# Moving the side work of four token tiles between ScalarE, VectorE and GpSimd in a two-layer kernel, and starting row scores two places sooner

## The reference, cut to what matters

```python
x = x + tanh(g_xattn[0]) * align(ctx_1024, layernorm(x))       # time warping against 1500 rows of a context
x = x + tanh(g_ffn[0])   * memory(layernorm(x), w_q, keys, w_down, w_up)
x = x + tanh(g_xattn[1]) * attention(layernorm(x), ctx_1024, ctx_1024, Wq, bq, Wk, bk, Wv, bv, Wo, bo)
x = x + tanh(g_ffn[1])   * experts(layernorm(x), W_router, b_router, W1, b1, W2, b2)

# memory: 8 heads, product keys (2 x 32), the best of 1024 experts each
h = einsum('bnd,bnhkd->bnhk', x, w_down[indices])
h = gelu(h, approximate=False) * relu(scores)
y = einsum('bnhk,bnhkd->bnd', h, w_up[indices])
# attention: 16 heads of 8, 56 queries against 1500 keys of the same batch
attn = softmax(einsum('bhqd,bhkd->bhqk', Q, K) / sqrt(8)); y = einsum('bhqk,bhkd->bhqd', attn, V) @ Wo + bo
```

## Time and profile before

| | us |
|---|---|
| median of three runs | 536.01 (534.08 to 536.66) |
| profiled execution | 540.89, of which the span from first to last instruction is 539.1 |
| PE busy | 435.2 (81%) |
| DVE busy | 366.1 (68%) |
| ACT busy | 281.9 (52%) |
| POOL busy | 86.0 (16%) |

### The profile page before, as it was taken

The page is one execution under the profiler, slowest core; times in us unless marked ns, Lnnn a source line. Parts: engine busy times, 40 slices in busy tenths (PEclk is TensorE's granted clock), DMA queues, the critical chain, the costliest instruction groups (busy, mean ns, idle before and its releaser), DMA issues.

```text
span 539.1 us, 10292 instructions
## 1 busy us (share of the span) xinstructions
PE 435.2 (81%) x4039; PEld 264.2 (49%) x4039; DVE 366.1 (68%) x1008; ACT 281.9 (52%) x491; POOL 86.0 (16%) x105
## 2 busy tenths in 40 slices
PE   3997888667888887257577568999989999989996
PEld 1343333335555574135445435666656566544443
DVE  7557999998666795868864757778869883371112
ACT  4365888755422591524245216466746567634443
POOL 2000000000000007777502602021010211100000
PEclk9999999998999999569797859799999999989999
DMA  8500565334522105486100780346273481000000
GB/s 287 213 2 0 154 195 163 118 101 122 170 68 64 52 3 117 113 203 150 34 1 1 162 183 2 72 103 149 53 146 85 90 283 34 2 0 0 1 0 18
DMA packets 28720, 50.07 MB, mean 93 GB/s; under 512 B 2464, under 2 KB 18400, under 8 KB 28672
## 3 DMA queue, kind: packets, MB, share of 16 engines
q1 hardware_dynamic: 26848, 45.74, 31.5%
q0 software_dynamic: 1536, 3.67, 2.7%
q10 hardware_dynamic: 288, 0.00, 0.0%
HBM read 39.96 MB, written 9.45 MB: 92 GB/s over the span
## 4 chain that ended last, share of the span: by engine, by line
PE 51%; DVE 30%; issue 6%; DMA 4%; POOL 4%; ACT 4%; SPq 1%; DVEq 0%; POOLq 0%
PE banks L1720 8%; PE banks L1696 8%; PE banks L1768 6%; PE banks L1832 5%; DVE arena L1320 5%; DVE work L1349 4%; PE banks L1846 4%; DVE mx L1103 3%; DVE arena L1373 2%; DMA arena<-key_parts 2%; PE banks L1408 2%; PE banks L1546 2%; PE banks L1662 2%; DVE work L1315 2%; PE banks L1412 2%
## 5 line engine op out<-in xcount | busy, mean ns | idle before, releaser
L1103 DVE TENSOR_REDUCE mx<-banks 112x1 f32<-112x500 f32 x168 | 107.9, 676 | 35.1 <-PE banks L1696 34.5
L851 ACT ACTIVATE arena<-banks 128x896 f32<-128x896 f32 x96 | 87.9, 916 | 69.1 <-PE banks L1768 68.0
L1696 PE MATMUL banks<-ctxT,arena 128*112 128x500 bf16 x144 | 56.4, 412 | 9.5 <-DVE mx L1103 6.6
L1720 PE MATMUL banks<-arena 128*32 128x112 f32 (+1 forms) x1536 | 60.6, 275 | 4.2 <-issue 3.3
L1430 PE MATMUL banks<-steps,one 128*128 128x500 f16 (+1 forms) x149 | 42.3, 357 | 11.1 <-DVE hcol L1049 10.5
L1720 PEld LDWEIGHTS banks<-arena 128*32 128x32 f32 (+1 forms) x1536 | 35.4, 112 | 25.6 <-issue 22.9
L1768 PEld LDWEIGHTS banks<-arena,ctxT 128*128 128x128 bf16 (+1 forms) x576 | 40.5, 110 | 12.0 <-issue 5.5
L1768 PE MATMUL banks<-arena,ctxT 128*128 128x112 bf16 (+1 forms) x576 | 44.6, 223 | 0.0
L1349 DVE SCALAR_TENSOR_TENSOR work<-twice,banks,arena 128x202 f32<-128x202 f32 x68 | 29.5, 434 | 18.8 <-PE banks L1546 18.8
L1320 DVE TENSOR_TENSOR_SCAN arena<-work,arena 128x100 f32<-128x100 f32 x70 | 29.8, 426 | 7.4 <-ACT work L663 5.0
L1469 PE MATMUL banks<-arena,minusb 128*128 128x375 bf16 x64 | 20.0, 331 | 17.8 <-ACT arena L672 15.0
(11 more groups left out here) (288 smaller groups left out, 760.5 us busy)
## 6 DMA issues: line engine op xcount, KB each, us to landing
ctxT<-key_parts SPq DMA_DIRECT2D x36, 375.0 KB, 6.3
key_parts<-arena SPq DMA_DIRECT2D x32, 281.2 KB, 2.8
ctxT<-in_ctx_T SPq DMA_DIRECT2D x12, 500.0 KB, 9.0
arena<-key_parts SPq DMA_DIRECT2D x12, 375.0 KB, 7.5
ctxT<-in_ctx_nat SPq DMA_DIRECT2D x5, 750.0 KB
arena<-in_ctx_nat SPq DMA_DIRECT2D x3, 750.0 KB
arena<-in_L_ffn_W SPq DMA_DIRECT2D x1, 2048.0 KB, 9.1
arena<-in_fold_w SPq DMA_DIRECT2D x1, 768.0 KB, 5.7
```

The source lines that it names most:

```text
L851: nc.scalar.activation(Pt[0:rows, g % 2, :].rearrange("p (a n) -> p a n", a=2), banks[0:rows, 2 + 2 * (g % 2):4 + 2 * (g % 2), 0:HQ // 2], ...
L1103: nc.vector.tensor_reduce(mx3[:, b % 2, u // NPIECE, u % NPIECE:u % NPIECE + 1], ps[k % 2][0:2 * NJ, 0:PIECE], AX_X, ALU.max).then_inc(s_m ...
L1696: nc.tensor.matmul(ps[k % ring][0:2 * NJ, 0:PIECE], QP[:, u // NPIECE, b, :], KP[b % 3][:, u // NPIECE, (u % NPIECE) * PIECE:(u % NPIECE + ...
L1720: last = nc.tensor.matmul(ps[6 + b % 2][q:q + 32, o:o + 2 * NJ], vals[0:rows, v0:v0 + 32], Pt[0:rows, g % 2, 2 * t * NJ:2 * (t + 1) * NJ], ...
```

## The change

- POOL clears `picks` where it filled the ones below key parts 0; ACT fills those ones instead of those below key parts 1, and lays `picks`, which DVE did. POOL fills the ones of key parts 1 later. Row scores no longer read the rows of ones (96 partitions instead of 128), so only the chunks wait for them.
- DVE lays the gates of tiles 0 and 1 in one operation each, where ACT did it in eight. The order on DVE becomes: tokens of tile 0, products of tile 1, query split of tile 0.
- Tiles 0 and 1 get their deviation from ACT's square root and DVE's reciprocal; ACT loads the tables of Sqrt and Gelu in turn for that. Tiles 2 and 3 get moments and a first guess on DVE, twelve Newton operations and the normalization on POOL.
- POOL splits the queries of tiles 1 to 3.
- Gelu of tiles 2 and 3 comes before the table of Exp, their memory output after chunk 2; the query rows of tile 1 come in chunks 5 to 8 of batch 0.
- `LEAD` is 6.

```diff
     MAXROW_AT = 10
-    LEAD = 4
+    LEAD = 6
     MAXROW = [NCH - 1] + (NB - 1) * [MAXROW_AT]
     DUE = [min(2 * g + 4, UNITS) if g < NCH else min(UNITS + 3 * (g - NCH + 1), 2 * (g + 1) + LEAD, (NB - 1) * UNITS)
            for g in range(NB * NCH)]
     assert all(DUE[b * NCH + MAXROW[b] - 1] >= (b + 1) * UNITS for b in range(NB - 1))
-    DOT_AT, GATE_AT, TOK_AT = (3, 6), 10, 18
-    NORM_AT, SPLIT_AT = (0, 2), 20
-    TURN_C, QUERY_C, LAY_C = 5, 7, 5
-    GELU_C, MEMORY_C = 4, 8
+    N_ROOT = 12
+    GATE_AT, TOK_AT, STAT_AT = 1, 10, 12
+    MEMORY_C, TURN_C, QUERY_C, LAY_C = 2, 5, 7, 5
...
-            nc.gpsimd.memset(ctxT[NPR:P, 0:KPW], 1.0 + 0x3F80 / 2.0 ** 23).then_inc(s_one[0], 1)
-            pool.wait_ge(s_one[0], 1)
+            nc.gpsimd.memset(picks, 0.0).then_inc(s_pz, 1)
+            pool.wait_ge(s_pz, 1)
...
+            def split_queries(i, t, nt):
+
+                q = Qm[:, 0:nt, :]
+                pool.wait_ge(s_qh, i + 1)
+                nc.gpsimd.tensor_tensor(q, q, QS[:, t:t + nt, 0, :], ALU.subtract).then_inc(s_rt, 1)
+                pool.wait_ge(s_rt, 1 if i == 1 else N_ROOT + 3)
+                nc.gpsimd.tensor_copy(QS[:, t:t + nt, 1, :], q).then_inc(s_rt, 1)
+                pool.wait_ge(s_rt, 2 if i == 1 else N_ROOT + 4)
+                nc.gpsimd.tensor_tensor(QS[:, t:t + nt, 2, :], q, QS[:, t:t + nt, 1, :], ALU.subtract).then_inc(s_qs, 1)
+
+            pool.wait_ge(s_gm, 2)
+            split_queries(1, 1, 1)
...
+            nc.gpsimd.memset(ctxT[NPR:P, KPW:2 * KPW], 1.0 + 0x3F80 / 2.0 ** 23).then_inc(s_one[1], 1)
+            pool.wait_ge(s_one[1], 1)
+            pool.wait_ge(s_vr, 3)
+            half, y, a = (ln[:, 2:4, i] for i in (8, 9, 10))
+            roots = 2
+
+            def root(ins):
+                nonlocal roots
+                roots += 1
+                ins.then_inc(s_rt, 1)
+                pool.wait_ge(s_rt, roots)
+
+            for _ in range(3):
+                root(nc.gpsimd.tensor_tensor(a, y, y, ALU.mult))
+                root(nc.gpsimd.tensor_tensor(a, a, half, ALU.mult))
+                root(nc.gpsimd.tensor_scalar(a, a, 1.5, None, ALU.subtract))
+                root(nc.gpsimd.tensor_tensor(y, y, a, ALU.mult))
+            for t in (2, 3):
+                if t == 3:
+                    pool.wait_ge(s_x2, 3)
+                nc.gpsimd.tensor_scalar(x_tok[:, t, :], x1_tok[:, t, :], ln[:, t, 6:7], ln[:, t, 9:10], ALU.subtract,
+                                        ALU.mult).then_inc(s_x2, 1)
+            pool.wait_ge(s_x2, 4)
...
+                if b == 1:
+                    split_queries(2, 2, 2)
+                    pool.wait_ge(s_qs, 3)
...
+            nc.scalar.activation(ctxT[NPR:P, 0:KPW], two1[NPR:P, 0:1].broadcast_to([P - NPR, KPW]), ACT.Copy
+                                 ).then_inc(s_one[0], 1)
+            act.wait_ge(s_pz, 1)
+            own = ident[:, :].rearrange("p (m r) -> p m r", r=G)
+            for c, (_, qx) in enumerate(PRODUCTS):
+                nc.scalar.activation(picks[:, :, qx, c::len(PRODUCTS)], own, ACT.Copy).then_inc(s_picks, 1)
...
+            gelu(0)
+            nc.scalar.activation(warm[:, 2:3], epsc[:, :], ACT.Sqrt)
+            token_deviation(0)
+            nc.scalar.activation(warm[:, 3:4], epsc[:, :], ACT.Gelu)
+            lay_tokens(0, 0, ps[7])
+            mask_queries(0, 0, ps[6])
+            gelu(1)
+            for p in range(NH // 4):
+                query_rows(0, p)
+            nc.scalar.activation(warm[:, 4:5], epsc[:, :], ACT.Sqrt)
+            token_deviation(1)
+            nc.scalar.activation(warm[:, 5:6], epsc[:, :], ACT.Gelu)
+            lay_tokens(1, 1, ps[7])
+            mask_queries(1, 1, ps[6])
...
-            nc.scalar.activation(warm[:, :], epsc[:, :], ACT.Exp)
             maxima_rows(0)
+            gelu(2)
+            gelu(3)
+            nc.scalar.activation(warm[:, 6:7], epsc[:, :], ACT.Exp)
...
-                    if b == 0 and c == GELU_C:
-                        gelu(2)
-                        gelu(3)
-                        nc.scalar.activation(warm[:, :], epsc[:, :], ACT.Exp)
...
-                    if b in (2, 3) and LAY_C <= c < LAY_C + NH // 4:
-                        query_rows(b, c - LAY_C)
+                    if b in (0, 2, 3) and LAY_C <= c < LAY_C + NH // 4:
+                        query_rows(b or 1, c - LAY_C)
...
+            def lay_gates(t):
+                ve.wait_ge(s_hs, t + 1)
+                nc.vector.tensor_tensor(
+                    diag[t], ident[0:TT, 0:TT].unsqueeze(1).broadcast_to([TT, NHK, TT]),
+                    hcol[:, t, :].unsqueeze(2).broadcast_to([TT, NHK, TT]), ALU.mult).then_inc(s_dg, 1)
+
+            def token_moments(t):
+                link(nc.vector.bn_stats(ln[:, t, 0:6], x1_tok[:, t, :]))
+                return nc.vector.bn_aggr(ln[:, t, 6:8], ln[:, t, 0:6])
...
+                ve.wait_ge(s_sr, t + 1)
+                link(nc.vector.reciprocal(ln[:, t, 9:10], ln[:, t, 8:9]))
+                nc.vector.tensor_scalar(x_tok[:, t, :], x1_tok[:, t, :], ln[:, t, 6:7], ln[:, t, 9:10], ALU.subtract,
+                                        ALU.mult).then_inc(s_x2, 1)
...
+            def guess_roots():
+
+                var, half, y = (ln[:, 2:4, i] for i in (7, 8, 9))
+                link(nc.vector.tensor_scalar(half, var, EPS, 0.5, ALU.add, ALU.mult))
+                nc.vector.tensor_scalar(y.bitcast(I32), half.bitcast(I32), -0.5, -554214945.0, ALU.mult, ALU.add
+                                        ).then_inc(s_vr, 1)
...
                 gates(0)
-                lay_picks()
+                lay_gates(0)
                 ve.wait_ge(s_x1c, 2)
                 add_memory(0)
+                token_moments(0).then_inc(s_vr, 1)
                 normalize_tokens(0)
-                split_queries(0, 0)
                 down(1)
+                split_queries()
+                gates(1)
+                ve.wait_ge(s_up, 1)
+                lay_gates(1)
...
                     reduce_pair(m)
-                    if m == 1:
-                        gates(1)
                     if m == 3:
                         add_memory(1)
+                        token_moments(1).then_inc(s_vr, 1)
+                    if m == 4:
                         normalize_tokens(1)
-                    if m == 5:
-                        split_queries(1, 1)
                 for step in range(7):
                     ve.wait_ge(s_dve, n)
                     split_maxima(0, step)
+                sum_dots(2)
+                sum_dots(3)
                 for k in range(UNITS, NB * UNITS):
                     b, u = k // UNITS, k % UNITS
-                    if b == 1 and u in DOT_AT:
-                        sum_dots(2 + DOT_AT.index(u))
                     if b == 1 and u == GATE_AT:
                         gates(2)
                         gates(3)
                     if b == 1 and u == TOK_AT:
                         add_memory(2)
                         add_memory(3)
-                    if b == 2 and u in NORM_AT:
-                        normalize_tokens(2 + NORM_AT.index(u))
-                    if b == 2 and u == SPLIT_AT:
-                        split_queries(2, 2)
+                    if b == 1 and u == STAT_AT:
+                        link(token_moments(2))
+                        link(token_moments(3))
+                        guess_roots()
                     reduce_scores(b, u)
...
                 if u == 0:
                     for half in range(2):
                         pe.wait_ge(s_kpl[b % 3][half], 16 * len(PRODUCTS) // 2 * (b // 3 + 1))
-                    if b < 3:
-                        pe.wait_ge(s_one[b], 1)
...
-            pe.wait_ge(s_qs, 2)
-            for p in range(NH // 4):
-                query_rows(1, p)
-            pe.wait_ge(s_qpa, NH // 2)
+            pe.wait_ge(s_qh, 2)
+            pe.wait_ge(s_xl, 2)
...
+                    if b == 0 and LAY_C <= c < LAY_C + NH // 4:
+                        pe.wait_ge(s_qs, 2)
+                        pe.wait_ge(s_vr, 3)
+                        query_rows(1, c - LAY_C)
```

110 lines of the change are left out of this document (42 added, 68 removed).

## The result

The changed kernel took 522.13 us in the median of four runs (518.82 to 522.59), the kernel before 536.34 on the same chip (534.08 to 539.32): ratio 0.973 [0.967, 0.979]. That is 14.2 us less; 23.7 were forecast. A second set of runs on another chip gave 522.48 beside 537.41, 14.9 less; its six runs spread from 513.53 to 526.51.

What follows compares the result with a forecast made beforehand. PE was taken as bound by waits for DVE's maxima, a table load and key parts, with half clock behind the gaps. Savings 6.2 + 5.2 + 5.0 + 5.6 + 1.7 = 23.7 us gave median 512.3, range 503 to 526.

Steps and rivals of the forecast that it cites:

- first rival: POOL's work holds up DVE at tile 1's norm, batch 0's split maxima and boundary casts: six us, 518; chance 0.15.
- half clock: PE stays at half clock through batch 1, 38.8 us instead of 25.8: 525; chance 0.12.
- A: From the gathers to batch 0's split maxima: earlier gathers and work taken off DVE save 6.2 us, between 1.5 and 7.5.
- B: Batch 0 and just ahead of it: waits, half clock and filling matmuls go, query rows of tile 1 enter; 5.2 us saved.
- C: Boundary from batch 0 to 1: earlier memory output ends the key-part load wait; 9.3 us become 4.3, saving 5.0.
- D: Batch 1: late tiles' norms and query split leave DVE, LEAD 6; 31.4 us become 25.8, saving 5.6.
- kept ACT from the exponentials: Batch 0: gelu pair and two table loads occupy ACT 3.1 us; removal ends PE's 2.77 wait and 2.7 of half clock.
- 6 x 1.47: Batch 1: its last six chunks, of two units each, run at full clock, 1.47 us each.
- Later: From batch 2 on: row-score units a chunk sooner remove 0.35 us before transposes at five boundaries, saving 1.7.
- I take the same gain off both: Profiled execution 540.89 to timed median 536.01: the 4.9 us difference was assumed to hold after the change, 517.2 to 512.3.
- an effect missing altogether: POOL's gates or the key-part load come as late as before elsewhere, and PE waits there: 535; chance 0.03.
- a slower kernel: PE's clock stays at 0.50 from batch 1 through batch 3, each chunk costing 1.17 us more: 554; chance 0.04.

Runs made afterwards that it cites:

- tables and a wait: Changed kernel with a gelu pair and its two table loads back behind batch 0's chunk 4, and DVE waiting for the second gelu before row-score unit 10: 524.93 us.
- POOL apart: Changed kernel with POOL's query splits waiting for DVE's splits of maxima, and the expert layer's fills and selects moved behind them: 513.49 us.
- four places: Changed kernel with LEAD 4 instead of 6, so row-score units are four places ahead: 516.79 us.
- a guard: POOL apart with four places, plus POOL's first product of gathered rows waiting until DVE has normalized tile 1: 507.35 us.

## Why the prediction was right, and where not

The time of 522.13 lies inside the range of 503 to 526, but outside the forecast's own 508 to 517: it stands between the first rival's 518 and the half clock's 525. The trace came closer, 22.0 us saved of 23.7, and part of that is luck. In the four parts below, the gain put down was 0.5 too large, 2.6 too small, 2.8 too large and 1.0 too large; the two large errors cancel.

**To the first transposes, forecast 7.9 (A, and the 1.7 that B takes off ahead of the loop), 7.4 measured.** The gathers left at 216.49 (216.2 forecast), the first maxima stood at 247.02 (247.0), the split ended at 264.58 (264.1). The steps hold, among them that tile 1's product eats most of what the earlier gathers give. The Trainium skill (ScalarE: Activation LUTs, "What ACT_TABLE_LOAD costs") would have A 1.4 smaller by a drain beside each load; ACT's operations in the run with tables and a wait (1.28, 0.20, 0.19, 1.28 and 0.20 us between 280.67 and 283.77) have no room for it either.

**Batch 0, forecast 4.3 (the rest of B, and 0.8 of C), 6.9 measured.** The gelu's part was sized rightly, 5.1 against 5.5, and explained wrongly: the failed step is "kept ACT from the exponentials". The rows of ACT showed it busy, and I took that for the cause; DVE's row at 285.46, which I had not drawn on, showed who was waiting. The query rows cost 0.58 in each of four chunks (2.05 from one group to the next instead of 1.47) and one wait of 0.43, 2.7 against 3.4. The memory output came with no wait before it. What no term had is that PE's small waits for maxima earlier in the batch shrink. The waits of 272 to 283 us before and of 265 to 290 after have (total, times, longest):

```profile
PE banks L1696 <- DVE mx L1103: 2.0, 5, 0.9
```
```profile
PE banks L1740 <- DVE mx L1151: 0.7, 3, 0.3
```

With the wait for the transposes (2.15, where 2.4 was kept) these come to some 2 of the 2.6; the rest is not told apart.

**The boundary and batch 1, forecast 9.8, 7.0 measured.** From the last values (290.65 + 0.59) to the first scores at 294.95 it is 3.7 (4.3 forecast). The load is no longer waited for, and sent late it costs 4.9: C holds. D had 25.8 from first scores to first scores and it took 29.4 (294.95 to 324.35). The half clock behind the boundary lasted about 7 us, in which the values of two chunks stand 3.1 apart (296.70 and 299.79): little more than the two chunks of 3.0 that I had let it. The step of D that failed is the "6 x 1.47" for the last six chunks, in which nothing holds PE: the wait of 2.38 with its own half clock was in no term. Its mechanism is my first rival's, at a place that I had not listed: six places put DVE's split of batch 2 on the very time at which POOL splits the late queries. With POOL apart the part is 11.5 us at full clock (35.02 to 23.48), more than forecast, and 9.2 with the half clock behind the boundary (35.02 to 25.81). The rule of the Trainium skill that one port pair serves DVE and POOL and is held for a whole instruction (SBUF — State Buffer, "SBUF: two separate sides") fits this: the traces of the changed kernel and its variants agree in that the held DVE operations end 0.02 to 0.10 us behind POOL's instruction. They don't agree in that whoever starts first holds it: by the profile's times one of DVE's began 0.19 before POOL's and was held all the same (last section).

**Later, forecast 1.7, 0.7 measured, and not by the pace.** Between the transposes from batch 2 on, four places and six come out alike. The 0.35 us at a boundary is given back in waits for maxima (2.9 us in five behind 325 us in the trace after).

**From the trace to the time: the step that failed most.** "I take the same gain off both", 4.9 us, put the profiled execution of the changed kernel above its median as that of the kernel before was. It was 3.3 below. That alone, 4.9 and 3.3, is 8.2 of the 9.8 us by which 512.3 missed. What the traces of one code show of the spread: POOL's first fill began anywhere from 204.75 to 208.97, though nothing ahead of it was changed; the norm of tile 1 was held in four of the eleven traces of the changed order without a guard (1.59 to 2.75 us instead of 0.34 to 0.50), and the first transposes were 2.0 to 3.3 us later in these, though not by the hold alone (with four places and POOL not apart, 2.5 of the 3.3 stood already at the first maxima); and a gap in batch 4 (below) costs some 3 to 5. Both profiled executions of the changed kernel itself were free of the held norm. So my first rival, at the first of its places, is a loss that comes and goes from one execution to the next, and the trace pair did not show it. How often it comes in the timed runs, which have no trace, stays open.

Of the other rivals, the half clock did not hold through batch 1: it was over after about 7 us and came back for the last few. Neither an effect missing altogether nor a slower kernel was seen.
